# A two-block MetaFormer on one core: last attention-input rows and first FFN norm kept on chip, gathers and small loads in other places

## The reference, cut to what matters

```
x = x + attention(ln_c(x))               # block 0
t = tokens(x);  t = t + ffn(ln_t(t))     # 4 experts, 96 -> 384 -> 96, gates of the top 2
x = x + conv7(ln_c(x))                   # block 1: 7x7 + 5x3 + 3x5 + 7x1*1x7 + 5x1*1x5, depthwise
t = tokens(x);  t = t + ffn(ln_t(t))

attention(x):                            # value, query: depthwise 3x3; key, off: 3x3, stride 2
  o      = gelu(layernorm(off) * ln_g + ln_b)
  pos    = tanh(einsum(o, w_off2) + ref)             # one sampling position for each of 28x28 points
  v      = bilinear sample of value at pos           # four corners, gathered by index
  attn   = einsum(query, key) * SCALE;  out = einsum(attn, v);  y = einsum(out, w_out)
ffn(x): out = sum_e gate_e(x) * (gelu(x @ w1_e + b1_e) @ w2_e + b2_e)
```

## Time and profile before

| | |
|---|---|
| median of the runs | 1711.93 us |
| profiled execution, its own time | 1717.21 us |
| its span, first to last instruction | 1715.4 us |
| PE / PEld busy | 1422.9 / 958.6 us (83% / 56%) |
| DVE / ACT / POOL busy | 979.1 / 701.8 / 275.8 us |
| mean granted TensorE clock | 0.943 of full speed |
| DMA | 137.96 MB, mean 80 GB/s |
| chain that ended last | PE 50%, issue 19%, DVE 12%, POOL 8%, ACT 5%, DMA 3% |

### The profile page before, as it was taken

One profiled execution on the slowest core, in us unless ns is written; L12 is line 12 of the kernel. 1 busy time (PEld: TensorE's weight loads), 2 busy tenths in 40 slices (PEclk: granted clock), 3 DMA queues, 4 the chain that ended last, 5 costly groups with the idle time before them and its releaser, 6 DMA issues.

```text
span 1715.4 us, 19469 instructions
## 1 busy us (share of the span) xinstructions
PE 1422.9 (83%) x6076; PEld 958.6 (56%) x6076; DVE 979.1 (57%) x2678; ACT 701.8 (41%) x1433; POOL 275.8 (16%) x190
## 2 busy tenths in 40 slices
...
GB/s 100 129 95 46 105 20 116 53 111 57 90 120 52 122 67 51 95 112 61 106 103 59 129 67 52 93 120 70 71 64 114 98 66 48 71 69 42 69 61 45
DMA packets 169448, 137.96 MB, mean 80 GB/s; under 512 B 114688, under 2 KB 163074, under 8 KB 168962
## 3 DMA queue, kind: packets, MB, share of 16 engines
...
## 4 chain that ended last, share of the span: by engine, by line
PE 50%; issue 19%; DVE 12%; POOL 8%; ACT 5%; DMA 3%; SPq 2%; ACTq 1%; POOLq 0%; DVEq 0%
PE y_ps L917 19%; PE at_ps L1020 8%; POOL pix_mem L837 6%; PE h_ps L926 5%; PE h_ps L925 5%; PE h_ps L924 5%; DVE vq_mem L1195 4%; PE at_ps L973 3%; POOL ln_rstd L824 3%; ACT ln_cen L689 2%; PE lb_ps L894 2%; PE lg_ps L907 1%; DVE part L1151 1%; DVE kon_mem L1195 1%; ACT hidden L784 1%
## 5 line engine op out<-in xcount | busy, mean ns | idle before, releaser
L784 ACT ACTIVATE hidden<-h_ps,b 128x448 f32<-128x448 f32 x672 | 424.6, 634 | 716.9 <-PE h_ps L926 714.0
L917 PE MATMUL y_ps<-hidden,w 128*96 128x448 f32 x1344 | 638.0, 559 | 29.6 <-ACT hidden L784 21.3
L924 PE MATMUL h_ps<-xh,w1h 96*128 96x448 f32 x672 | 474.4, 706 | 0.0
L1151 DVE SCALAR_TENSOR_TENSOR part<-y_ps,b,gate_t 96x448 f32<-96x448 f32 x224 | 151.8, 678 | 512.4 <-PE y_ps L917 472.4
L824 POOL TENSOR_TENSOR ln_rstd<-ln_ve,minus_half 112x4 f32<-112x4 f32 x112 | 156.0, 1393 | 1208.9 <-DVE ln_ve L1134 1208.7
L917 PEld LDWEIGHTS y_ps<-hidden,w 128*96 128x96 f32 x1344 | 207.4, 167 | 105.0 <-ACT hidden L784 59.5
L925 PE MATMUL h_ps<-xl,w1h 96*128 96x448 f32 x672 | 250.7, 373 | 0.0
L926 PE MATMUL h_ps<-xh,w1l 96*128 96x448 f32 x672 | 249.2, 371 | 0.0
L924 PEld LDWEIGHTS h_ps<-xh,w1h 96*128 96x128 f32 x672 | 130.5, 194 | 139.2 <-issue 122.9
L925 PEld LDWEIGHTS h_ps<-xl,w1h 96*128 96x128 f32 x672 | 131.8, 196 | 120.5 <-issue 119.7
L689 ACT ACTIVATE ln_cen<-ln_cen,ln_rstd 112x96 f32<-112x96 f32 x448 | 130.2, 363 | 160.7 <-POOL ln_rstd L824 160.5
...
## 6 DMA issues: line engine op xcount, KB each, us to landing
gate_t<-gates_dram SPq DMA_DIRECT2D x112, 336.0 KB, 3.1
value_pairs<-pix_mem SPq DMA_DIRECT2D x56, 168.0 KB, 3.1
...
ln_x<-in_x SPq DMA_DIRECT2D x28, 168.0 KB, 2.5
norm_a<-ln_cm SPq DMA_DIRECT2D x28, 168.0 KB, 2.3
...
```

Of the source, the lines that this page charges most:

```text
L784: act.activation(hidden[c % HID_RING][:, :], h_ps[c % H_BANKS][:, 0:TILE], ACT.Gelu, bias=b1[l][:, c:c + 1]).then_inc(gelu_done, 1)
L917: pe.matmul(y_ps[e % Y_BANKS][0:C, 0:TILE], w2[l][:, c, :], hidden[c % HID_RING][:, :], start=(j == 0), stop=(j == CPE - 1)).then_inc(hid_ ...
L924: pe.matmul(ps, hi, xh[:, ring(k)], start=True, stop=False)
L1151: dve.scalar_tensor_tensor(part[:, e, :], y_ps[e % Y_BANKS][0:C, 0:TILE], b2[l][:, e:e + 1], gate_t[e // 2][:, e % 2, :], ALU.add, ALU.mul ...
```

## The change

1. **Attention input.** For images 0, 2 and 3 (`DIRECT`) the last norm tile (rows 48 to 55) isn't stored to DRAM: three transfers put it from `ln_cm` into the last quarter of `xq`. The fourth quarter load is split into the rows before and the padding row. The quarter loads stand elsewhere between the stores. Image 1 keeps the old way.
2. **FFN norm of image 0.** Its seven jobs (all in the start stage) are turned by PE straight out of `x_res`; their loads from `x_attn` fall away. The load of `x_res` for image 1 waits until all seven are turned.
3. **Gathers.** The 16 of an image go 4 behind stage 3, 4 and 5 in stage 4, 3 in stage 5, instead of 2, 4, 4, 6.
4. **Small loads.** ACT issues 9 loads at its start instead of 23; SP issues four of the others behind the first two `ln_x` loads, six behind (-1, 0), and the last four, with `w_out` and `q_mask`, at the end of (-1, 1).
5. **Preparations.** `expand_w_out` and `spread_w_out` go from (-1, 4) to the end of (-1, 8), `fold_taps` from (1, 0) to the same place behind it.

```diff
@@ -94,6 +94,7 @@
     LATE[_step] = [job for job in JOBS[STEPS[_i - 1]] if job.place == 1] if _i > 0 else []
+DIRECT = (0, 2, 3)
 GATE_TILES = ((0, 4), (4, TILES))
@@ -391,7 +395,16 @@
         def norm_stores(norm, parity, tiles=TILES):
-            return 16 * sum(job.norm == norm and job.n % 2 == parity and job.tile < tiles for job in PLACED)
+            return 16 * sum(job.norm == norm and not direct(job) and job.n % 2 == parity and job.tile < tiles for job in PLACED)
+
+        def direct(job):
+            return job.norm is not None and job.norm[0] == "a" and job.norm[1] in DIRECT and job.tile == TILES - 1
+
+        def from_attn(job):
+            return job.kind == "f" and job.step[0] < 0
+
+        def loads(n):
+            return 16 * sum(job.n % 2 == n % 2 and not from_attn(job) for job in PLACED[:n + 1])
@@ -443,8 +463,16 @@
+            def load_tap_rows(n):
+                with nc.allow_non_contiguous_dma("small"):
+                    for dst, src in tap_rows[:n]:
+                        sp.dma_start(dst, src).then_inc(taps_ld, 16)
+                del tap_rows[:n]
+
             def load_norm(n):
                 job = PLACED[n]
+                if from_attn(job):
+                    return
                 if n >= 2:
@@ -468,6 +496,11 @@
                     sp.wait_ge(ln_moved, job.n + 1)
+                    if direct(job):
+                        for g in range(G):
+                            sp.dma_start(xq[Q - 1::Q, g, LAST_ROW * SIDE:LAST_ROW * SIDE + TILE],
+                                         ln_cm[job.n % 2][32 * g:32 * g + 32, :]).then_inc(xq_direct, 16)
+                        return
                     if k == "a":
@@ -482,10 +515,12 @@
                     sp.wait_ge(at_free, AT["conv", 0] + FILLS)
+                split = b in DIRECT and q == Q - 1
                 for i in range(2):
-                    sp.wait_ge(norm_st["a", b, i], norm_stores(("a", b), i, QUARTER_TILES[q]))
-                sp.dma_start(xq[q::Q], norm["a"][b].rearrange("(g c) n -> c g n", g=G)[
-                    :, :, q * QPIX:q * QPIX + ROWS_A * SIDE]).then_inc(xq_ld, 16)
+                    sp.wait_ge(norm_st["a", b, i], norm_stores(("a", b), i, TILES - 1 if split else QUARTER_TILES[q]))
+                for r0, r1 in ((0, LAST_ROW), (ROWS_A - PAD_A, ROWS_A)) if split else ((0, ROWS_A),):
+                    sp.dma_start(xq[q::Q, :, r0 * SIDE:r1 * SIDE], norm["a"][b].rearrange("(g c) n -> c g n", g=G)[
+                        :, :, q * QPIX + r0 * SIDE:q * QPIX + r1 * SIDE]).then_inc(xq_ld, 16)
@@ -590,14 +626,20 @@
                     load_norm(coming[0].n)
-                if slot < 0 and p in (2, 3):
-                    load_quarter(0, p - 2)
-                if 0 in stages:
-                    for q in range(2 if slot < 0 and p == 4 else 0, Q if slot < 0 else 3):
-                        load_quarter(stages[0], q)
+                if slot < 0 and p == 3:
+                    load_quarter(0, 0)
+                    load_quarter(0, 1)
+                if 0 in stages and stages[0] > 0:
+                    for q in range(Q):
+                        if q < 2 or slot < 0:
+                            load_quarter(stages[0], q)
                 for job in LATE[slot, p]:
                     store_norm(job)
+                if slot < 0 and p == 3:
+                    load_quarter(0, 2)
+                    load_quarter(0, 3)
                 if 0 in stages and slot >= 0:
+                    load_quarter(stages[0], 2)
                     load_quarter(stages[0], 3)
@@ -609,6 +651,10 @@
                             sp.wait_ge(attn_st[q], 16 * b)
+                    if b == 1:
+                        for job in PLACED:
+                            if from_attn(job):
+                                sp.wait_ge(ln_turned, job.n + 1)
                     sp.dma_start(x_res[:, :], x_in[b]).then_inc(xres_ld, 16)
@@ -632,7 +678,14 @@
                     store_attn(stages[6], 3)
+                if (slot, p) == (-1, 0):
+                    load_tap_rows(9)
                 if (slot, p) == (-1, 1):
+                    with nc.allow_non_contiguous_dma("small"):
+                        sp.dma_start(ref_pos[:, :], a["c_ref_pos"]).then_inc(w_out_ld, 16)
+                        sp.dma_start(ln_gb[:, 0], a["L0_conv_ln_g"].partition_broadcast(HPTS)).then_inc(w_out_ld, 16)
+                        sp.dma_start(ln_gb[:, 1], a["L0_conv_ln_b"].partition_broadcast(HPTS)).then_inc(w_out_ld, 16)
+                        sp.dma_start(w_off2[:, :], a["L0_conv_w_off2"].partition_broadcast(HPTS)).then_inc(w_out_ld, 16)
                     sp.dma_start(w_out[:, :], a["L0_conv_w_out"]).then_inc(w_out_ld, 16)
@@ -663,23 +716,12 @@
                 act.dma_start(dst, src).then_inc(taps_ld, 16)
-                taps_count[0] += 1
...
                 load(to_quarters[:, :], a["c_to_quarters"])
-                r_w_a, r_b_a, r_w_c, r_w53, r_w35, r_w7, r_w5, r_b_c = views(rows_w)
                 for n, w in enumerate(("v", "k", "off1", "q")):
...
                     load(r_b_a[:, n], a[f"L0_conv_b_{w}"].rearrange("(g c) -> c g", g=G))
-                for dst, w in ((r_w_c, "w77"), (r_w53, "w53"), (r_w35, "w35"), (r_w7[:, 0], "w7h"),
-                               (r_w7[:, 1], "w7w"), (r_w5[:, 0], "w5h"), (r_w5[:, 1], "w5w")):
-                    load(dst, a[f"L1_conv_{w}"].rearrange("(g c) o h w -> c g (o h w)", g=G))
-                for n, w in enumerate(("b77", "b53", "b35")):
-                    load(r_b_c[:, n], a[f"L1_conv_{w}"].rearrange("(g c) -> c g", g=G))
-                load(ref_pos[:, :], a["c_ref_pos"])
-                load(ln_gb[:, 0], a["L0_conv_ln_g"].partition_broadcast(HPTS))
-                load(ln_gb[:, 1], a["L0_conv_ln_b"].partition_broadcast(HPTS))
-                load(w_off2[:, :], a["L0_conv_w_off2"].partition_broadcast(HPTS))
@@ -697,6 +739,8 @@
                     act.wait_ge(split, f_count(before) + 1)
+                elif before is not None and direct(before):
+                    act.wait_ge(xq_direct, 16 * G * (DIRECT.index(before.image) + 1))
                 elif before is not None:
@@ -848,15 +892,15 @@
                 if 4 in stages:
-                    gather(stages[4], 2, 6)
+                    gather(stages[4], 4, 8)
                 if 5 in stages:
-                    gather(stages[5], 10, 2 * GQ)
+                    gather(stages[5], 13, 2 * GQ)
                 if 1 in jobs:
...
                 if 3 in stages:
-                    gather(stages[3], 0, 2)
+                    gather(stages[3], 0, 4)
                 if 4 in stages:
-                    gather(stages[4], 6, 10)
+                    gather(stages[4], 8, 13)
@@ -877,11 +921,16 @@
                 n = job.n
-                pe.wait_ge(ln_loaded[n % 2], 16 * (n // 2 + 1))
+                src = ln_x[n % 2]
+                if from_attn(job):
+                    src = x_res[:, tile_cols(job.tile)]
+                    pe.wait_ge(at_free, AT["attn", 0] + AT_Y + -(-(job.tile + 1) * TILE // YCOL))
+                else:
+                    pe.wait_ge(ln_loaded[n % 2], loads(n))
                 if n > 0:
...
                 for s in range(NSUB):
-                    last = pe.transpose(lt_ps[0:SUB, s * C:(s + 1) * C], ln_x[n % 2][:, s * SUB:(s + 1) * SUB],
+                    last = pe.transpose(lt_ps[0:SUB, s * C:(s + 1) * C], src[:, s * SUB:(s + 1) * SUB],
                                         ident[0:C, 0:C])
@@ -1029,8 +1078,6 @@
                     pe.wait_ge(split, TILES * u + p + 1)
-                if (slot, p) == (-1, 4):
-                    spread_w_out()
                 for c in range(CHUNKS):
@@ -1059,6 +1106,8 @@
                     second(TILES * u + p, FFN[u][0], CHUNKS - 1)
+                if (slot, p) == (-1, 8):
+                    spread_w_out()
                 if (slot, p) == (-1, 2):
@@ -1431,7 +1481,6 @@
                     dve.wait_ge(taps_set, 1)
-                    expand_w_out()
                 if by_stage.get(0) == 3:
@@ -1451,7 +1500,8 @@
                     if at == 0 and till > 0 and 0 in by_stage:
-                        dve.wait_ge(xq_ld, 16 * Q * (by_stage[0] + 1))
+                        dve.wait_ge(xq_ld, 16 * XQ_LOADS[by_stage[0]])
+                        dve.wait_ge(xq_direct, 16 * G * sum(image <= by_stage[0] for image in DIRECT))
                     for op in ops[at:till]:
@@ -1494,7 +1544,8 @@
                     split_weights()
-                if (slot, p) == (1, 0):
+                if (slot, p) == (-1, 8):
+                    expand_w_out()
                     fold_taps()
```

More of the change, by code:

```diff
@@ L341, in metaformer_kernel @@
         xq_ld = sem("xq_ld")
+        xq_direct = sem("xq_direct")
         a_step = sem("a_step")
@@ L380, in metaformer_kernel @@
         LEAD_APPLY, LEAD_BACK, LEAD_MOVE, LEAD_SCORES, LEAD_LATE_MOVE = (3, 8), 8, 9, 10, 4
-        const_count, taps_count = [0], [0]
+        const_count = [0]
         BAND_TILES = [3, 4, 6, 7]
```

(14 more changed lines are left out.)

5 lines of the change are left out of this document (3 added, 2 removed).

## The result

| | median | runs | ratio to the kernel before |
|---|---|---|---|
| before | 1712.43 us | 1710.65 to 1713.68 (4) | |
| after | 1699.64 us | 1696.97 to 1703.34 (4) | 0.9924, 95% interval 0.9901 to 0.9946 |

Forecast was 1698, range 1686 to 1708. The gain is 12.8 us at the medians. The profiled execution of after took 1696.97, its span is 1694.8 against 1715.4: 20.6 less, since it was its kernel's fastest run and that of before slower than every run in this table.

A forecast was written before the change was run, and what follows sets the result against it. PE bounds the kernel from about 540 us; the edits act earlier and in image 3's attention, on waits of DVE, ACT and PE. Terms sum to -14.4 us: 1711.93 to 1697.5, said as 1698; 8-in-10 range 1686 to 1708.

The forecast's parts named there:

- Start: Up to image 0's first taps: small loads, w_out moved and direct rows bring them from 46.22 to 40.3; -5.9 us, kept.
- Both preparations: At (-1, 8) on DVE: w_out 5.8 plus fold_taps 6.3, less 4.5 hidden in the wait for image 1's quarters; +7.6 us.
- rival D: The block at (-1, 8) isn't hidden at all, image 1's quarters being late too: costs 12.1; total -9.9, 1702.0; chance 0.12.
- Two gathers in the start stage: On POOL before the job at 254.29: two more gathers cost 5.7 us where POOL was idle 4.79; +0.9 us.
- Image 1: Fifth gather delays the power that ACT awaits by 2.0 us; DVE's 3.68 wait for the last gathers goes; -1.7 us.
- Image 2: Around 510 to 528 us: fold_taps gone -6.3, fifth gather +2.9, DVE's wait for last gathers gone -4.7; -8.1 us.
- Image 3: Gathers near 920 us: same reckoning as image 1, with a removed wait of 4.99 at 920.37; -3.0 us.
- Last rows: Before the taps of images 2 and 3: quarter loads leave without waiting for the store; -2.2 and -2.0 us.
- FFN norm from x_res: Image 0's FFN norm: 7 loads and three store waits fewer, but hardly any wait was a load; 0, bounds -2 to 0.
- Rival A: SP is the bound of the start and quarters: start gives 2, last rows 0; total -6.3, 1705.6; chance 0.15.
- Rival B: PE's clock stays at 2.4 GHz behind shorter waits, some 6 us more at five places; total -20.4, 1691.5; chance 0.13.
- Rival C: Gathers come no earlier: their waits stay, the fifth gather holds ACT 3.4 in each image; total +4.0, 1716; chance 0.05.

## Why the prediction was right, and where not

- **Start, -5.9.** First taps 5.8 earlier, every mark on the way within 0.6. "DVE is full from there on, so this is kept" failed: 0.5 was kept. The tile jobs among the taps need loads too, and I read SP's list only up to the first taps. The row of 12 constants behind it was in the trace of before; moving them gave 6.5 back. So DVE wasn't full "from there on": 5.4 of the 5.9 were lost to a wait that the sum doesn't have, and the first FFN matmul came 7.6 later than before (274.62 against 267.01), not the 2 to 4 that were to show the prediction right.
- **Both preparations, +7.6.** Measured 7.6. The gap hid its 4.5, so rival D (12.1) is out.
- **Two gathers in the start stage, +0.9.** Tile 1 of after against the old gathers: +0.4.
- **Image 1, -1.7.** From +7.2 to +5.5 at tile 2: -1.7, as forecast; ACT waited 1.0 longer and not 2. Another 2.0 followed at tile 3, not in the sum.
- **Image 2, -8.1.** Keys and values start 7.5 earlier at 525.05 (532.56 before), from +1.1: -8.6. Behind it 1.5 more to tile 10, in a stretch where the clock was up (0.93 from 500 to 550 against 0.76); with the old gathers 0.9 of it comes too.
- **Image 3, -3.0.** Tile 23: -2.5 from tile 22. Another 3.2 follow at tile 24 and aren't in the sum; the old gathers have 1.3 of them.
- **Last rows, -2.2 and -2.0.** Tiles 4 and 18: -2.5 and -2.7; by the run without them only 0.7 and 1.4. Mis-sized by half.
- **FFN norm from x_res, 0.** Held for the change.
- **Rival A**: SP was a bound of the start, but by the constants and not by the small loads; with those on ACT it is 5.9 slower. **Rival B** is in part what happened, surely at tile 3 (2.0), and less surely at tile 10 (1.5). **Rival C** is out: three gathers behind the last power took 3.3, 1.0 and 1.0 in image 1.

So 1698 came out by luck, in that two errors cancel: 5.4 too much in the start, and about 4 too little in the rest, 12.8 against 14.4 - 5.4 = 9.0. The runs say it more plainly. The gathers' terms were 5.6 in all (image 2's without the 6.3 of fold_taps), and they are worth 7.8 alone and 12.6 in the changed kernel. All the other terms were 8.8 in all, and with the old gathers all the other changes together measure nothing (1712.2, as before). The forecast put most of the gain on the half of the change that gives none by itself.

What each part is worth as the kernel stands, by taking it back: gathers 12.6, fold 1.3, direct rows 1.2, norm from x_res 1.2, w_out -2.7; their sum, 13.6, is near the 12.8 of the change, but the small loads and image 0's direct rows are not in it, and the three of 1.2 and 1.3 are too small for the times to tell from nothing. That a single part put into before is worth 7.8 and taken from after 12.6 shows that they don't add. Why they don't is open. The clock has 3.5 us of it in image 1 and, by PE's busy time, 2.2 of 14.4 in all in one pair of traces, where PE's busy time spreads by 12.3 over all of them.

The port lock that the Trainium skill describes ("SBUF — State Buffer", Who interferes with whom) was set against 3.37 in the prediction. After has a plainer row, the power of 12.71: it starts 0.3 ahead of thirteen tap operations of 1.0 and less and ends 0.9 behind the last. By the page the loser is held for one instruction of the other; here the power, which had begun first, was held for the whole row.
